# Decoder block on one core: narrow attention heads on quarters of the TensorE array

## The chip, the cores and the metric

The kernel runs on one core of one Trainium2 chip. The metric is device microseconds of one execution. The kernel before takes 4916.42 us (median of 3 runs, 4914.16 to 4921.12).

## The reference

A two-layer decoder over x of shape 4 x 512 x 256 (four batches): attention with 16 heads of 64, layer norm, attention of x against a context with 16 heads of 16 and a mask, layer norm, a mixture of 8 experts, layer norm, a four-layer state-space scan, layer norm, a second cross-attention with 8 heads of 32, and a quantized gated network. The change touches only the two cross-attentions. Their core, cut from the reference (all in float32):

```python
# first cross-attention: H = 16, D_K = 16
q = proj(query, Wq, bq); k = proj(key, Wk, bk); v = proj(key, Wv, bv)
scores = einsum('bhqd,bhkd->bhqk', q + pos_bias, k + pos_bias) / sqrt(D_K)
scores = where(m == 0, -1e9, scores)
out = einsum('bhqk,bhkd->bhqd', softmax(scores), v)
# second cross-attention: H = 8, d = 32
a = softmax(einsum('bhnd,bhmd->bhnm', qh, kh) / sqrt(d))
ca = einsum('bhnm,bhmd->bhnd', a, vh)
```

## The kernel before, in words

All engines run hand-written programs that meet in semaphores. For each batch the kernel does three attention passes with one routine, `attend`, written once for each engine: pass A (16 heads of 64, 32 steps), pass B (16 heads of 16, padded to 32, 32 steps), and, late in the kernel, pass E (8 heads of 32, 16 steps). The passes A and B of the four batches lie in the first 1.4 ms, those of E in the last 0.8 ms. The experts and the scan lie between.

One step is two heads and one tile of 128 queries against all 512 keys. On TensorE (`attend` at L1034) step i issues, in this order: the scores of step i (L1046, two products of 128 queries by 512 keys into two PSUM banks, `PS[:, 2 * (i % 2) + q]`), the eight 128x128 transposes of the probabilities of step i - 3 (L1058), and the value products of step i - 7 (L1075). In pass B and E (`per == 4`) a head has 32 rows and 32 columns. Its scores are still computed with 64 rows of the array: q is stored twice (`pj_q`, L731 to L738), once with the odd and once with the even 32-row strips set to zero, so that one 64-row product gives one head. The two heads of a step use rows 0 to 63 and 64 to 127. The value products of a head write 32 of the 128 columns (`p0`), over 512 queries, for one chunk c of 128 keys:

```python
for q in range(2):
    h = head(j, q, per)
    p0 = h % per * wide
    ins = pe.matmul(PS[p0:p0 + wide, 6 + bank % 2, :], V[:, c, h * wide:(h + 1) * wide],
                    pT[j % 2][:, q, c, :], start=c == 0, stop=c == 3)
```

The other engines in step i: VectorE (`attend` at L1437) takes the row maximum of the scores (pass B: two masked reductions L1451 that also copy the scores into `b_S`, then `nm` at L1454; pass E: one reduction L1459), copies half of the transposed probabilities of step i - 3 out of PSUM bank 4 (L1466) and takes the reciprocal of the sums of step i - 1 (L1477). ScalarE (`attend` at L744) takes the two exponentials of step i (L754) and copies the other half, bank 5, of step i - 3 (L764). GpSimd multiplies the probabilities by the reciprocals (L590). The order is fixed by hand: each engine runs these in the order named, and waits where its input is missing. TensorE waits for `probs_ok` of step i - 2 before the scores, for `scaled` (GpSimd) and for `pt_a`, `pt_v` (both copies of the step before) before the transposes. ScalarE waits for `smax` (L1454 or L1459) before the exponentials, and for the transposes before its copy.

Before a pass, TensorE projects q (L1022) and ScalarE writes it to SBUF: with `pj_q` in two activations for each of 4 (B) or 2 (E) tiles. The first scores of the pass wait for the last of them. After the pass VectorE copies the last bank (L1483) and TensorE goes on with transposes (L1131) or the output projection (L1030).

Of the kernel before, what the change touches and what calls it, by code (L numbers as in the profile page):

```python
# [25 lines left out]
P = 128  # L26
# [73 lines left out]
def decoder(nc, d, out):  # L100
# [11 lines left out]
    with ExitStack() as ctx:  # L112
# [34 lines left out]
        rden = sb("rden", [P, 4, 2])  # L147
        strip01 = sb("strip01", [P, 2])
        qs_b = sb("qs_b", [P, 2])
        qs_e = sb("qs_e", [P, 2])  # L150
        qb_b = sb("qb_b", [P, 2, 4])
        qb_e = sb("qb_e", [P, 2, KC])
        from80 = sb("from80", [P, 1])
# [211 lines left out]
        def head(j, q, per):  # L365

            return 2 * j + q if per == 2 else 4 * (j // 2) + j % 2 + 2 * q

# [347 lines left out]
        def _(act):  # L716
# [13 lines left out]

            def pj_q(b, u, qT, c, nc, scale, bias):  # L731


                act.wait_ge(pj_ps, PJ(b, u) + 1)
                for k in range(2):
                    ins = act.activation(qT[:, k * nc + c, :], PS[:, u % 4, :], ACT.Identity,
                                         bias=bias[:, k, c:c + 1], scale=scale[:, k:k + 1])
                ins.then_inc(pj_ev, 1)  # L738

            def ln(b, i):  # L740
                act.wait_ge(ln_mv, LN(b, i) + 1)
                act.activation(std[:], mv[:, :, 1], ACT.Sqrt, bias=epsc[:, 0:1]).then_inc(ln_std, 1)

            def attend(b, at, n, src, zero_key, probs, pT):  # L744
                s0, g0 = AT(b, at), GT(b, at // 4)
                for i in range(n + LAG):
                    if i < n:
                        s = s0 + i
                        act.wait_ge(smax, s + 1)
                        if i >= 4:  # L750
                            act.wait_ge(pt_ps, s - 3)
                            act.wait_ge(den_ok, s - 3)
                        for q in range(2):
                            ins = act.activation(probs[:, i % 4, q, :], src(i, q), ACT.Exp,  # L754
                                                 bias=nm[:, i % 4, q:q + 1], accum_out=sm[:, i % 4, q:q + 1])
                        if zero_key:
                            ins = act.activation(e0[:, i % 4, :], nm[:, i % 4, :], ACT.Exp)
                        ins.then_inc(probs_ok, 1)
                    k = i - LAG
                    if k >= 0:  # L760
                        act.wait_ge(pt_ps, s0 + k + 1)
                        if k % 4 == 0 and k >= 8:
                            act.wait_ge(av, g0 + k // 4 - 1)
                        act.activation(pT[k // 4 % 2][:, 1, :, k % 4 * P:(k % 4 + 1) * P],  # L764
                                       PS[:, 5, :].rearrange("p (c q) -> p c q", q=P), ACT.Copy).then_inc(pt_a, 1)

# [16 lines left out]
            def attention(b):  # L783
                attend(b, AT_A, 32, lambda i, q: PS[:, 2 * (i % 2) + q, :], True, probs, pT)
# [7 lines left out]
                attend(b, AT_B, 32, lambda i, q: b_S[:, i % 2, q, :], False, probs, pT)  # L792
                ln(b, 1)
                tr_ev(TR_LNB, XT[:, 0, :], b)
# [170 lines left out]
            with act.Fori(0, B) as b:  # L965
# [10 lines left out]
                for c in range(KC):  # L976
                    pj_q(b, PJ_EQ + c, s_qT, c, KC, qs_e, qb_e)
                attend(b, AT_E, 16, lambda i, q: PS[:, 2 * (i % 2) + q, :], False, e_probs, e_pT)
                ln(b, 5)
# [23 lines left out]
        def _(pe):  # L1003
# [29 lines left out]

            def attend(b, at, n, qT, kT, V, per, ot, probs, pT, between=None):  # L1034
                s0, g0, o0 = AT(b, at), GT(b, at // 4), OT(b, ot)
                wide = 64 if per == 2 else 32
                for i in range(n + LAG + 4):
                    if i < n:
                        s, t = s0 + i, i % T
                        if i >= 2:  # L1040
                            pe.wait_ge(probs_ok, s - 1)
                        for q in range(2):
                            h = head(i // T, q, per)
                            r = 64 * q
                            part = h % 2 * (qT.shape[1] // 2) if per == 4 else 0
                            ins = pe.matmul(PS[:, 2 * (i % 2) + q, :],  # L1046
                                            qT[r:r + 64, part + h // per, t * P:(t + 1) * P],
                                            kT[r:r + 64, h // per, :], start=True, stop=True)
# [12 lines left out]
                    if k == n and between is not None:  # L1061
                        between()
                    x = i - LAG - 4
                    if x >= 0:
                        j, c = x // 4, x % 4
                        bank = j if per == 2 else j // 2
                        if c == 0:
                            pe.wait_ge(pt_a, s0 + 4 * j + 4)
                            pe.wait_ge(pt_v, s0 + 4 * j + 4)
# [35 lines left out]
            def attention(b):  # L1105
# [7 lines left out]

                attend(b, AT_A, 32, a_qT, a_kT, a_V, 2, OT_A, probs, pT, keys)
                for t in range(T):
# [11 lines left out]
                pe.wait_ge(tm_ev, TM.one(b, TM_SA))  # L1127
                attend(b, AT_B, 32, b_qT, b_kT, b_V, 4, OT_B, probs, pT)
                for t in range(T):
# [170 lines left out]
            with pe.Fori(0, B) as b:  # L1300
# [26 lines left out]
                pe.wait_ge(tm_ev, TM.two(b, TM_MHA))  # L1327
                attend(b, AT_E, 16, s_qT, s_kT, s_V, 4, OT_E, e_probs, e_pT)
                for t in range(T):
# [43 lines left out]
        def _(v):  # L1373
            v.wait_ge(ld_const, 64)
            for g in range(4):
                for k in range(2):
                    v.memset(strip01[32 * g:32 * g + 32, k:k + 1], 1.0 if g % 2 == k else 0.0)

            v.wait_ge(act_set, 1)
# [7 lines left out]
            v.wait_ge(r_init, 5)  # L1387
            for k in range(2):
                v.tensor_scalar(qb_b[:, k, :], cols[:, C_BQ:C_BQ + 4], strip01[:, k:k + 1], None, ALU.mult)
                v.tensor_scalar(qb_e[:, k, :], cols[:, C_QB:C_QB + KC], strip01[:, k:k + 1], None, ALU.mult)  # L1390
            v.tensor_scalar(qs_b[:], strip01[:], 0.25, None, ALU.mult)
            v.tensor_scalar(qs_e[:], strip01[:], 32.0 ** -0.5, None, ALU.mult).then_inc(dve_set, 1)
            v.wait_ge(dve_set, 1)
# [43 lines left out]
            def attend(b, at, n, own, per, ot, zero_key, out_T, masked, pT):  # L1437
                s0, g0 = AT(b, at), GT(b, at // 4)
                for i in range(n + LAG + 5):
                    s = s0 + i  # L1440
                    if i < n:
# [4 lines left out]
                        if masked:  # L1446
# [3 lines left out]
                            for q in range(2):  # L1450
                                ins = v.tensor_tensor_reduce(b_S[:, i % 2, q, :], PS[:, 2 * (i % 2) + q, :], b_neg[:, i % T, :],  # L1451
                                                             1.0, -3.0e38, ALU.add, ALU.max, mx[:, i % 4, q:q + 1])
# [9 lines left out]
                    if 0 <= k < n:  # L1462
                        v.wait_ge(pt_ps, s0 + k + 1)
                        if k % 4 == 0 and k >= 8:
                            v.wait_ge(av, g0 + k // 4 - 1)
                        v.tensor_copy(pT[k // 4 % 2][:, 0, :, k % 4 * P:(k % 4 + 1) * P],  # L1466
                                      PS[:, 4, :].rearrange("p (c q) -> p c q", q=P)).then_inc(pt_v, 1)
                    k = i - 1
# [432 lines left out]
```

## Time and profile before

| | us |
|---|---|
| median of 3 runs | 4916.42 |
| profiled execution | 4919.05 |
| its span, first to last instruction | 4917.4 |
| TensorE busy | 4034.2 (82%) |
| VectorE busy | 3272.3 (67%) |
| ScalarE busy | 2190.4 (45%) |
| GpSimd busy | 2323.4 (47%) |
| mean granted TensorE clock | 0.924 |

The profiled execution is 2.6 us above the median, and 1.65 us of it lie outside the span. A product in float32 appears as two MATMUL records of its form, each with its weight load (PEld); a transpose appears as one. The busy time of matmuls is modelled at their ends, so the start of the next group is the better measure of what a group costs. [...]

### The profile page before, as it was taken

To read this page: it belongs to the slowest core of one execution; us is meant where nothing else is said; L and a number is where in the kernel's file an instruction comes from. 1 tells how busy PE (TensorE), PEld (TensorE's weight loads), DVE (VectorE), ACT (ScalarE), POOL (GpSimd) and SP (SyncE) were. 2 spreads that over 40 slices of the span, in tenths; PEclk is the share of its full clock that TensorE was granted. 3 is DMA by queue.
4 is the path that set the end of the run, shared out by engine and by line. 5 is a ranking of instruction groups with operands and counts; after the bars stand their busy time and mean duration, and the time that the engine had idled before them with its cause. 6 is when DMAs were issued, how large, how long until landed. Compare 5 with 4: busy or idle time off the path is not lost.

```text
span 4917.4 us, 47718 instructions
## 1 busy us (share of the span) xinstructions
PE 4034.2 (82%) x14992; PEld 2056.3 (42%) x14992; DVE 3272.3 (67%) x4305; ACT 2190.4 (45%) x4097; POOL 2323.4 (47%) x1202
## 2 busy tenths in 40 slices
PE   7888888888869995888888888888889866776766
PEld 3433443444359992333333333333333323333433
DVE  3555446445631114999999999999999995454454
ACT  3444445434522224555555545555555542242332
POOL 2344334324410006777777777777777773120210
PEclk9999999999979996999999999998999999887988
DMA  5000000000068862111111111111111111000000
GB/s 205 18 5 10 18 14 1 18 14 9 1 240 319 311 267 78 33 31 36 41 33 35 33 42 31 35 33 42 31 38 34 33 60 37 1 13 13 0 5 4
DMA packets 102371, 272.72 MB, mean 55 GB/s; under 512 B 9776, under 2 KB 55728, under 8 KB 96400
## 3 DMA queue, kind: packets, MB, share of 16 engines
q1 hardware_dynamic: 97216, 256.75, 15.3%
q0 software_dynamic: 4944, 13.51, 0.8%
q8 instruction: 90, 1.47, 0.1%
q14 instruction: 121, 0.99, 0.1%
HBM read 237.32 MB, written 32.90 MB: 55 GB/s over the span
## 4 chain that ended last, share of the span: by engine, by line
PE 55%; POOL 15%; issue 13%; DVE 10%; ACT 4%; SPq 1%; DMA 1%; POOLq 0%; DVEq 0%; ACTq 0%
POOL AR L697 10%; PE PS L1278 7%; PE PS L1075 6%; PE PS L1058 6%; PE PS L1046 6%; PE PS L1171 6%; PE PS L1022 5%; PE PS L1030 4%; PE PS L1223 4%; PE PS L1181 3%; PE PS L1198 2%; DVE AR L1717 2%; POOL AR L655 1%; DVE PS L1711 1%; ACT AR L754 1%
## 5 line engine op out<-in xcount | busy, mean ns | idle before, releaser
L697 POOL TENSOR_TENSOR AR<-AR 128x1024 f32<-128x1024 f32 x512 | 1205.6, 2357 | 557.4 <-DVE AR L1717 543.1
L590 POOL TENSOR_TENSOR AR<-AR,rden 128x1024 f32<-128x1024 f32 x320 | 605.7, 1893 | 1292.5 <-DVE rden L1477 1226.3
L1278 PE MATMUL PS<-AR,ident 128*128 128x512 f32 x2048 | 1078.6, 653 | 165.8 <-POOL AR L697 165.7
L1717 DVE TENSOR_TENSOR_SCAN AR<-AR,PS 128x1024 f32<-128x1024 f32 x512 | 1170.3, 2286 | 19.0 <-ACT AR L929 1.4
L929 ACT ACTIVATE AR<-AR,mcol 128x511 f32<-128x511 f32 x1024 | 667.8, 711 | 116.2 <-DVE AR L1717 65.7
L1711 DVE TENSOR_TENSOR PS<-AR,PS 128x1024 f32<-128x1024 f32 x512 | 628.6, 1228 | 57.7 <-PE PS L1264 23.1
L1278 PEld LDWEIGHTS PS<-AR,ident 128*128 128x128 f32 x2048 | 384.1, 201 | 670.9 <-issue 385.9
L1058 PE MATMUL PS<-ident,AR 128*128 128x128 f32 x2560 | 344.7, 278 | 122.2 <-issue 68.3
L1058 PEld LDWEIGHTS PS<-ident,AR 128*128 128x128 f32 x2560 | 276.5, 141 | 381.5 <-issue 361.7
L1046 PE MATMUL PS<-AR 64*128 64x512 f32 x1280 | 363.2, 648 | 54.2 <-ACT AR L754 24.0
L754 ACT ACTIVATE AR<-PS,nm 128x512 f32<-128x512 f32 x384 | 260.4, 683 | 291.9 <-DVE nm L1457 227.5
L1075 PE MATMUL PS<-AR 128*32 128x512 f32 (+1 forms) x1280 | 331.7, 608 | 0.0
L1022 PE MATMUL PS<-AR 128*128 128x512 f32 x608 | 295.7, 645 | 20.8 <-DVE AR L1406 10.7
L1171 PE MATMUL PS<-AR 128*128 128x128 f32 x2496 | 287.8, 277 | 8.5 <-ACT AR L811 8.5
L1171 PEld LDWEIGHTS PS<-AR 128*128 128x128 f32 x2496 | 287.4, 193 | 10.8 <-ACT AR L811 8.9
L1030 PE MATMUL PS<-AR 128*128 128x256 f32 (+1 forms) x896 | 241.2, 429 | 45.4 <-DVE AR L1508 18.0
L1451 DVE CUSTOM_DVE_ANT_0 AR<-PS,AR 128x512 f32<-128x512 f32 x256 | 166.7, 689 | 166.6 <-PE PS L1046 146.7
L1198 PE MATMUL PS<-AR 128*128 128x512 f32 x512 | 263.7, 640 | 6.3 <-ACT AR L866 2.1
L1466 DVE COPY AR<-PS 128x512 f32<-128x512 f32 x320 | 220.0, 687 | 73.0 <-PE PS L1058 71.8
L754 ACT ACTIVATE AR<-AR,nm 128x512 f32<-128x512 f32 x256 | 182.6, 714 | 175.1 <-DVE nm L1454 174.9
L1223 PE MATMUL PS<-AR 128*128 128x512 f32 x512 | 240.4, 593 | 3.0 <-ACT AR L870 2.3
L1656 DVE TENSOR_TENSOR AR<-PS,AR 128x512 f32<-128x512 f32 x78 | 53.9, 691 | 271.9 <-ACT AR L820 271.9
(254 smaller groups left out, 4836.7 us busy)
## 6 DMA issues: line engine op xcount, KB each, us to landing
AR<-in_xw SPq DMA_DIRECT2D x39, 3072.0 KB, 10.4
AR<-mid_cs SPq DMA_DIRECT2D x256, 256.0 KB, 3.3
mid_xs<-AR SPq DMA_DIRECT2D x32, 512.0 KB, 7.8
AR<-mid_xs SPq DMA_DIRECT2D x39, 128.0 KB, 9.6
mid_ys<-AR POOLq DMA_DIRECT2D x39, 128.0 KB, 7.9
AR<-in_ctx SPq DMA_DIRECT2D x8, 512.0 KB, 5.1
AR<-in_mask SPq DMA_DIRECT2D x4, 1024.0 KB, 5.4
mid_x<-AR SPq DMA_DIRECT2D x8, 512.0 KB, 3.0
```

The costliest lines, as they stand in the source:

```text
L590: pool.tensor_tensor(probs[:, i % 4], probs[:, i % 4], rden[:, i % 4, :].rearrange("p (q o) -> p q o", o=1).to_broadcast([P, 2, 512]), ALU ...
L697: pool.tensor_tensor(m_HC[:, W % 3], m_H[:, W % 3, :].rearrange("p (c s) -> p c s", c=2), m_cb[:, n % 4:n % 4 + 1, :].to_broadcast([P, 2, ...
L754: ins = act.activation(probs[:, i % 4, q, :], src(i, q), ACT.Exp, bias=nm[:, i % 4, q:q + 1], accum_out=sm[:, i % 4, q:q + 1])
L929: ins = act.activation(m_dA[:, W % 4, c, 1:512], m_dl[i % 2][:, cc, 1:512], ACT.Exp, scale=mcol[:, i // B, at:at + 1])
L1022: ins = pe.matmul(PS[:, u % 4, :], w[:, k, c * P:(c + 1) * P], xT[:, k, :], start=k == 0, stop=k == kc - 1)
L1046: ins = pe.matmul(PS[:, 2 * (i % 2) + q, :], qT[r:r + 64, part + h // per, t * P:(t + 1) * P], kT[r:r + 64, h // per, :], start=True, stop ...
L1058: ins = pe.transpose(PS[:, 4 + q, c * P:(c + 1) * P], probs[:, k % 4, q, c * P:(c + 1) * P], ident[:])
L1075: ins = pe.matmul(PS[p0:p0 + wide, 6 + bank % 2, :], V[:, c, h * wide:(h + 1) * wide], pT[j % 2][:, q, c, :], start=c == 0, stop=c == 3)
L1171: ins = pe.matmul(PS[:, bank, f * P:(f + 1) * P], w[:, kc, f0:f0 + P], x_T[:, kc, :], start=kc == 0, stop=kc == KC - 1)
L1278: ins = pe.matmul(PS[:, 2 * hf + c, :], ident[:], m_HC[:, W % 3, c, :], start=False, stop=n == NS - 1)
L1711: v.tensor_tensor(PS[:, 4:6, :], m_du[i % 2][:, 2 * hf:2 * hf + 2, :], PS[:, 6:7, :].to_broadcast([P, 2, 512]), ALU.mult).then_inc(d_bx, 1)
L1717: v.tensor_tensor_scan(m_H[:, W % 3, :], m_dA[:, W % 4].rearrange("p c s -> p (c s)"), PS[:, 4:6, :].rearrange("p c s -> p (c s)"), 0.0, A ...
```

## The change

1. The heads of a narrow pass are taken in another order: steps i and i + 1 are now the four heads of one quarter set at the same query tile (`step_of`). For `per == 4` TensorE issues the scores of steps i and i + 1 together at even i, four products with 32 rows each, one for each quarter of the array's rows and one for each of the four PSUM banks, and none at odd i.
2. Before such a group TensorE waits for the step i - 1 (instead of i - 2): in pass B for `smax`, since VectorE's copy frees the bank, in pass E for `probs_ok`.
3. The value products of one issue are four, one for each quarter of the columns, over 256 queries (two tiles) instead of two over 512. The buffer pT is viewed as 4 heads x 4 chunks x 256 queries for this (`part_of`), and both copies write into this view.
4. q is no longer stored twice: `pj_q` and its zero strips are gone, and q is written by one activation for each tile (`pj`).
5. Some tiny VectorE instructions of the set-up of those strips are gone. Pass A keeps its instructions and its order.

```diff
         def head(j, q, per):
-            return 2 * j + q if per == 2 else 4 * (j // 2) + j % 2 + 2 * q
+            return 2 * j + q
+        def step_of(i, per):
+            return (i // T, i % T) if per == 2 else (2 * (i // 8) + i % 2, i % 8 // 2)
+        def part_of(pT, k, q, per):
+            j, t = step_of(k, per)
+            if per == 2:
+                return pT[k // 4 % 2][:, q, :, t * P:(t + 1) * P]
+            quad = pT[k // 4 % 2].rearrange("p a c n -> p (a c n)").rearrange("p (h c n) -> p h c n", h=4, c=4)
+            return quad[:, 2 * (j % 2) + q, :, t % 2 * P:(t % 2 + 1) * P]
...
-            def pj_q(b, u, qT, c, nc, scale, bias):
-                act.wait_ge(pj_ps, PJ(b, u) + 1)
-                for k in range(2):
-                    ins = act.activation(qT[:, k * nc + c, :], PS[:, u % 4, :], ACT.Identity,
-                                         bias=bias[:, k, c:c + 1], scale=scale[:, k:k + 1])
-                ins.then_inc(pj_ev, 1)
...
-                    pj_q(b, PJ_BQ + c, b_qT, c, 4, qs_b, qb_b)
+                    pj(b, PJ_BQ + c, b_qT[:, c, :], ACT.Identity, 0.25, cols[:, C_BQ + c:C_BQ + c + 1])
...
                     if i < n:
-                        s, t = s0 + i, i % T
-                        if i >= 2:
+                        s = s0 + i
+                        free = smax if masked else probs_ok
+                        if per == 2 and i >= 2:
                             pe.wait_ge(probs_ok, s - 1)
-                        for q in range(2):
-                            h = head(i // T, q, per)
-                            r = 64 * q
-                            part = h % 2 * (qT.shape[1] // 2) if per == 4 else 0
-                            ins = pe.matmul(PS[:, 2 * (i % 2) + q, :],
-                                            qT[r:r + 64, part + h // per, t * P:(t + 1) * P],
-                                            kT[r:r + 64, h // per, :], start=True, stop=True)
-                        ins.then_inc(scores, 1)
+                        if per == 4 and i % 2 == 0 and i >= 2:
+                            pe.wait_ge(free, s)
+                        for e in ((i,) if per == 2 else (i, i + 1) if i % 2 == 0 else ()):
+                            j, t = step_of(e, per)
+                            for q in range(2):
+                                h = head(j, q, per)
+                                r = h % per * wide
+                                ins = pe.matmul(PS[:, 2 * (e % 2) + q, :], qT[r:r + wide, h // per, t * P:(t + 1) * P],
+                                                kT[r:r + wide, h // per, :], start=True, stop=True)
+                            ins.then_inc(scores, 1)
...
-                        for q in range(2):
-                            h = head(j, q, per)
-                            p0 = h % per * wide
-                            ins = pe.matmul(PS[p0:p0 + wide, 6 + bank % 2, :], V[:, c, h * wide:(h + 1) * wide],
-                                            pT[j % 2][:, q, c, :], start=c == 0, stop=c == 3)
+                        for q in range(per):
+                            h = per * bank + q
+                            p0 = q * wide
+                            n0 = 0 if per == 2 else u % 2 * 256
...
+                            ins = pe.matmul(PS[p0:p0 + wide, 6 + bank % 2, n0:n0 + 1024 // per], V[:, c, h * wide:(h + 1) * wide],
+                                            moved[:, q, c, :], start=c == 0, stop=c == 3)
```

TensorE's program in pass B of the kernel before, steps 5 to 7 (L1046 scores, L1058 transposes, L1075 value products; the REGISTER_ALU rows keep the semaphore counts):

```order
L1041 REGISTER_ALU
L1046 MATMUL PS<-AR 128x512 x2
L1058 MATMUL PS<-ident,AR 128x128 x8
L1041 REGISTER_ALU
L1046 MATMUL PS<-AR 128x512 x2
L1058 MATMUL PS<-ident,AR 128x128 x8
L1075 MATMUL PS<-AR 32x512 x2
L1041 REGISTER_ALU
L1046 MATMUL PS<-AR 128x512 x2
L1058 MATMUL PS<-ident,AR 128x128 x8
L1075 MATMUL PS<-AR 32x512 x2
```

The same place in the changed kernel (L1047 scores, L1058 transposes, L1078 value products):

```order
L1041 REGISTER_ALU
L1047 MATMUL PS<-AR 128x512 x4
L1058 MATMUL PS<-ident,AR 128x128 x8
L1052 REGISTER_ALU
L1058 MATMUL PS<-ident,AR 128x128 x8
L1078 MATMUL PS<-AR 32x256 x4
L1041 REGISTER_ALU
L1047 MATMUL PS<-AR 128x512 x4
L1058 MATMUL PS<-ident,AR 128x128 x8
L1078 MATMUL PS<-AR 32x256 x4
```

Every second step has lost its scores, and the step before it issues four. A value issue has four products of 256 instead of two of 512. The transposes stand where they stood.

ScalarE's program ahead of pass B, kernel before (writing q, with the semaphores waited for):

```order
L736 ACTIVATE AR<-PS,qb_b,qs_b 128x512 [waits pj_ps]
L736 ACTIVATE AR<-PS,qb_b,qs_b 128x512
L734 REGISTER_ALU
L736 ACTIVATE AR<-PS,qb_b,qs_b 128x512 [waits pj_ps]
L736 ACTIVATE AR<-PS,qb_b,qs_b 128x512
L749 REGISTER_ALU
L754 ACT_TABLE_LOAD
```

The changed kernel there:

```order
L736 ACTIVATE AR<-PS,cols 128x512 [waits pj_ps]
L735 REGISTER_ALU
L736 ACTIVATE AR<-PS,cols 128x512 [waits pj_ps]
L747 REGISTER_ALU
L752 ACT_TABLE_LOAD
```

One activation for each projected tile is left of two. The table load for the exponentials still follows the last of them.

## Rows read from the trace of the kernel before

**Rows 1.** The page: the group of the score products, all passes.

```profile
L1046 PE MATMUL PS<-AR 64*128 64x512 f32 x1280 | 363.2, 648 | 54.2 <-ACT AR L754 24.0
```

**Rows 2.** Whole passes B, E: length; PE, PEld, DVE, ACT, POOL busy; PEclk, DMA.

```profile
568.10:685.70 117.60, 98.90 (x513) 42.22 (x513) 73.19 (x228) 66.83 (x162) 60.57 (x32) 1.00 0.00 1
4757.40:4815.00 57.60, 49.58 (x258) 21.85 (x259) 32.60 (x50) 33.53 (x82) 30.29 (x16) 1.00 0.00 0
```

**Rows 3.** Chain that ended last, pass B: start, us, what.

```profile
600.67 1.06 PE PS L1046 x4
601.73 0.56 issue
602.30 1.06 PE PS L1058 x8
603.36 0.98 PE PS L1075 x4
...
605.40 0.20 issue
...
607.65 1.06 PE PS L1046 x4
```

**Rows 4.** Timeline, pass B, from the scores at 604.27 to the transposes at 609.29.

```profile
604.27 1.13 PE L1046 MATMUL PS<-AR 64*128 64x512 f32 x4
...
605.64 0.69 DVE L1451 CUSTOM_DVE_ANT_0 AR<-PS,AR 128x512 f32<-128x512 f32 x1 [1.48 <-PE PS L1046]
...
607.19 0.72 ACT L754 ACTIVATE AR<-AR,nm 128x512 f32<-128x512 f32 x1 [1.69 <-DVE nm L1454]
...
608.61 0.57 ACT L764 ACTIVATE AR<-PS 128x512 f32<-128x512 f32 x1
...
609.29 1.06 PE L1058 MATMUL PS<-ident,AR 128*128 128x128 f32 x8 [0.58 <-issue]
```

**Rows 5.** Chain that ended last, pass E.

```profile
4790.15 1.06 PE PS L1046 x4
...
4796.59 1.06 PE PS L1046 x4
```

**Rows 6.** Timeline of TensorE: second scores of a pass B, first and second of E.

```profile
572.58 1.13 PE L1046 MATMUL PS<-AR 64*128 64x512 f32 x4 [2.46 <-ACT AR L754]
...
4757.40 1.99 PE L1046 MATMUL PS<-AR 64*128 64x512 f32 x8 [1.62 <-ACT AR L736]
4761.33 1.13 PE L1046 MATMUL PS<-AR 64*128 64x512 f32 x4 [1.95 <-ACT AR L754]
```

**Rows 7.** Timeline of TensorE, the value products that end a pass E.

```profile
4809.07 4.57 PE L1075 MATMUL PS<-AR 128*32 128x512 f32 x20
```

**Rows 8.** Writing q (line L736), and a group of L729, one activation with a bias.

```profile
L736 ACT ACTIVATE AR<-PS,qb_b,qs_b x32: 768/774/779, 219.8 to 1243.5; 128x512 f32<-128x512 f32 x32
...
L729 ACT ACTIVATE AR<-PS,cols 128x512 f32<-128x512 f32 x64 | 44.0, 687 | 117.9 <-PE PS L1022 117.9
```

**Rows 9.** Stretches at the start of four passes (A, B, A, B); columns as in rows 2.

```profile
409.80:419.80 10.00, 7.59 (x28) 3.11 (x28) 6.78 (x14) 5.18 (x17) 3.78 (x2) 0.83 0.01 2
568.10:578.10 10.00, 6.31 (x28) 2.46 (x28) 7.16 (x24) 6.31 (x14) 3.78 (x2) 1.00 0.00 1
749.50:759.50 10.00, 6.40 (x28) 2.54 (x28) 7.23 (x14) 5.09 (x16) 3.78 (x2) 1.00 0.01 2
907.00:917.00 10.00, 7.07 (x26) 3.17 (x28) 6.27 (x23) 5.99 (x14) 3.79 (x2) 0.83 0.00 1
```

**Rows 10.** Timeline of TensorE in the last of those stretches.

```profile
911.45 1.13 PE L1046 MATMUL PS<-AR 64*128 64x512 f32 x4 [2.46 <-ACT AR L754]
913.05 1.93 PE L1046 MATMUL PS<-AR 64*128 64x512 f32 x4 [0.47 <-ACT AR L754]
914.91 1.93 PE L1058 MATMUL PS<-ident,AR 128*128 128x128 f32 x8
916.76 1.13 PE L1046 MATMUL PS<-AR 64*128 64x512 f32 x4
```

More of the change, by code:

```diff
@@ L147, in decoder @@
         rden = sb("rden", [P, 4, 2])
[L148 to L152, printed above, removed]
         from80 = sb("from80", [P, 1])
@@ L742, in ln, with attend @@
                 act.activation(std[:], mv[:, :, 1], ACT.Sqrt, bias=epsc[:, 0:1]).then_inc(ln_std, 1)
-            def attend(b, at, n, src, zero_key, probs, pT):
+            def attend(b, at, n, src, per, probs, pT):
                 s0, g0 = AT(b, at), GT(b, at // 4)
@@ L763, in attend @@
                             act.wait_ge(av, g0 + k // 4 - 1)
-                        act.activation(pT[k // 4 % 2][:, 1, :, k % 4 * P:(k % 4 + 1) * P],
-                                       PS[:, 5, :].rearrange("p (c q) -> p c q", q=P), ACT.Copy).then_inc(pt_a, 1)
+                        act.activation(part_of(pT, k, 1, per), PS[:, 5, :].rearrange("p (c q) -> p c q", q=P), ACT.Copy).then_inc(pt_a, 1)
             def project(b, prior=None):
@@ L783, in attention @@
             def attention(b):
-                attend(b, AT_A, 32, lambda i, q: PS[:, 2 * (i % 2) + q, :], True, probs, pT)
+                attend(b, AT_A, 32, lambda i, q: PS[:, 2 * (i % 2) + q, :], 2, probs, pT)
                 for c in range(4):
@@ L976, in _ @@
                 for c in range(KC):
-                    pj_q(b, PJ_EQ + c, s_qT, c, KC, qs_e, qb_e)
-                attend(b, AT_E, 16, lambda i, q: PS[:, 2 * (i % 2) + q, :], False, e_probs, e_pT)
+                    pj(b, PJ_EQ + c, s_qT[:, c, :], ACT.Identity, 32.0 ** -0.5, cols[:, C_QB + c:C_QB + c + 1])
+                attend(b, AT_E, 16, lambda i, q: PS[:, 2 * (i % 2) + q, :], 4, e_probs, e_pT)
                 ln(b, 5)
@@ L1032, in tm, with attend @@
                 ins.then_inc(tm_ps, 1)
-            def attend(b, at, n, qT, kT, V, per, ot, probs, pT, between=None):
+            def attend(b, at, n, qT, kT, V, per, ot, masked, probs, pT, between=None):
                 s0, g0, o0 = AT(b, at), GT(b, at // 4), OT(b, ot)
@@ L1064, in attend @@
                     if x >= 0:
-                        j, c = x // 4, x % 4
-                        bank = j if per == 2 else j // 2
+                        u, c = x // 4, x % 4
+                        bank = u if per == 2 else u // 2
                         if c == 0:
-                            pe.wait_ge(pt_a, s0 + 4 * j + 4)
-                            pe.wait_ge(pt_v, s0 + 4 * j + 4)
+                            pe.wait_ge(pt_a, s0 + 4 * u + 4)
+                            pe.wait_ge(pt_v, s0 + 4 * u + 4)
                             if bank >= 2:
                                 pe.wait_ge(o_sb, o0 + bank - 1)
-                        for q in range(2):
-                            h = head(j, q, per)
-                            p0 = h % per * wide
-                            ins = pe.matmul(PS[p0:p0 + wide, 6 + bank % 2, :], V[:, c, h * wide:(h + 1) * wide],
-                                            pT[j % 2][:, q, c, :], start=c == 0, stop=c == 3)
+                        for q in range(per):
+                            h = per * bank + q
+                            p0 = q * wide
+                            n0 = 0 if per == 2 else u % 2 * 256
+                            moved = (pT[u % 2] if per == 2 else
+                                     pT[u % 2].rearrange("p a c n -> p (a c n)").rearrange("p (h c n) -> p h c n", h=4, c=4))
+                            ins = pe.matmul(PS[p0:p0 + wide, 6 + bank % 2, n0:n0 + 1024 // per], V[:, c, h * wide:(h + 1) * wide],
+                                            moved[:, q, c, :], start=c == 0, stop=c == 3)
                         if c == 3:
@@ L1112, in keys @@
                         pj(b, PJ_BK + c, wbk, CT, c)
-                attend(b, AT_A, 32, a_qT, a_kT, a_V, 2, OT_A, probs, pT, keys)
+                attend(b, AT_A, 32, a_qT, a_kT, a_V, 2, OT_A, False, probs, pT, keys)
                 for t in range(T):
@@ L1127, in attention @@
                 pe.wait_ge(tm_ev, TM.one(b, TM_SA))
-                attend(b, AT_B, 32, b_qT, b_kT, b_V, 4, OT_B, probs, pT)
+                attend(b, AT_B, 32, b_qT, b_kT, b_V, 4, OT_B, True, probs, pT)
                 for t in range(T):
@@ L1327, in _ @@
                 pe.wait_ge(tm_ev, TM.two(b, TM_MHA))
-                attend(b, AT_E, 16, s_qT, s_kT, s_V, 4, OT_E, e_probs, e_pT)
+                attend(b, AT_E, 16, s_qT, s_kT, s_V, 4, OT_E, False, e_probs, e_pT)
                 for t in range(T):
@@ L1374, in _ @@
             v.wait_ge(ld_const, 64)
-            for g in range(4):
-                for k in range(2):
-                    v.memset(strip01[32 * g:32 * g + 32, k:k + 1], 1.0 if g % 2 == k else 0.0)
             v.wait_ge(act_set, 1)
@@ L1387, in _ @@
             v.wait_ge(r_init, 5)
[L1388 to L1392, printed above, removed]
+            v.sem_inc(dve_set, 1)
             v.wait_ge(dve_set, 1)
```

9 lines of the change are left out of this document (4 added, 5 removed).

## The prediction

> **What bounds the kernel now.** [...] The four passes B and four passes E are 700 us of the 4919.05; all else should stay. So the question is what a TensorE saving is worth inside a pass. The chain of waits answers it [rows 3]: two steps of pass B are scores 1.06, issue 0.56, transposes 1.06, values 0.98, scores 1.06, issue 0.20, transposes 1.06, values 0.98 = 6.98 us from 600.67 to 607.65. The two "issue" pieces are TensorE waiting ahead of the transposes. The timeline tells for what [rows 4]: scores start at 604.27, VectorE's reductions at 605.64, the exponentials at 607.19, ScalarE's copy L764 at 608.61, and 0.11 us after that copy has ended (609.18) the transposes start. From the scores to those transposes are 5.02 us, in which TensorE has a whole step of other work (1.06 + 0.98 + 1.06) and then waits. The period is this loop: 5.0 from scores to the next step's transposes, then 0.98 to 1.06 of transposes and 0.98 of values, and the scores of two steps later. Three of its parts belong to other engines. The reader is to see that TensorE is 6.2 of 6.98 us busy and yet that its work lies on the path only in part.
>
> **The change, part by part, against 4919.05.**
>
> *Scores.* Two groups of 1.06 become one group of four. The two products of a group run abreast: a record lasts 0.648 on the mean [rows 1], and the four of a group take 1.06 in all [rows 3]. I take 1.06 for four products as well; it can't be less than that, and two groups run apart would be 2.12. The removed group stood in the part of the loop where TensorE waits anyway, so alone it is worth nothing in the steady round; it turns into waiting.
>
> *Value products.* 0.98 for 512 columns in the middle of the stream; back to back, 20 records (five issues) take 4.57, the last four issues about 0.86 each [rows 7]. Half the columns stream in 0.43; with the 0.12 that an issue costs between other work, 0.55. Ends: 0.49 (half of 0.98) and 0.98 (the number of columns counts for nothing). One of the two issues in a round is in the loop. So the new loop of B is 5.02 + 0.99 + 0.55 = 6.56 us for two steps, 0.43 less than 6.98. VectorE is busy 73.19 / 32 = 2.3 us a step, ScalarE 2.1, GpSimd 1.9 [rows 2], so 4.6, 4.2 and 3.8 of the 6.56: none becomes the bound. The new wait for `smax` of step i - 1 is over before TensorE comes to it: 1.37 from scores to reductions and 1.55 for these and their negation [rows 4], some 0.8 of copy and reciprocal, 1.5 for the second reductions make 5.2, and the next group is due at 6.56. Pass E: 6.44 for two steps, from 4790.15 to 4796.59, becomes 6.0 by the same step [rows 5].
>
> *Whole passes.* B has 16 rounds, of which 12 are in the steady rhythm: 12 x 0.43 = 5.2. At the end of a pass nothing hides TensorE: the last scores fall away (1.06), and four value issues back to back are 0.43 shorter each: 2.8. The start of B is neutral: the second group waited for the first exponentials (2.46 idle [rows 6]) and now comes as late. Together 8.0, four times: 32 us. In E the second group starts 3.93 after the first [rows 6], now it must wait for the exponentials of the other step too, 1.4 (0.7 each, as in [rows 4]), of which I take 1.2, and so again in the next round: 2.4 lost. Three steady rounds give 1.3, the end 2.8: net 1.7, four times: 7 us.
>
> *Writing q.* The first scores wait for two activations of 0.774 behind the last projection; now for one of 0.687 [rows 8]: 0.86 less, eight times: 7 us. The removed activations of the other tiles lie beside the projections, the few set-up instructions beside the first loads: nothing.
>
> Sum so far: 32 + 7 + 7 = 46 us less.
>
> *What comes back: the clock.* In the new round of B TensorE works 1.06 + 0.99 + 0.55, then stands still for about 2.3 us until the copy frees the transposes, then works 1.54. Such a wait exists before only at the start of a pass, and there the clock answers: of four starts with an idle stretch of 2.2 to 2.5 us, two show a granted clock of 0.83 over 10 us and two show 1.00 [rows 9]. [...] I take 1.2. How often: half of the idle stretches of this size led to it, but a slowed round has no such idle stretch; so one in four of the 64 rounds of B, 16. In the steady rounds of E the wait is only about 1.8, and at 1.95 (the start of E) the clock held, so I count only the start of E, with an idle stretch of 4 us and one more behind it: 2 for a pass, 8. Together 24 x 1.2 = 29 us. Bounds: 8 of them (10 us) and one in almost every round, some 56 x 1.5 = 84 us.
>
> [...]
>
> Net: -46 + 29 = -17, from 4919.05 to 4902. The median lies 2.6 below the profiled execution: 4900.
>
> **The rivals.**
> 1. *The clock holds in pass B.* For it: half the starts held, and all steady rounds before did. Against: 64 new idle stretches. Then only E's starts cost 10: -36, 4880.
> 2. *The clock falls in nearly every round* (slower than before). The place is TensorE behind its wait for the ScalarE copy; price 1.5 for each fall, as more of the slowed work is then on the path; 84 us: 4954. It decides from 46 / 1.2 = 38 falls on, of some 96 rounds. Against it: a slowed group fills its own idle time.
> 3. *Quarters stream no faster by halving the columns*, since eight weight loads and eight products in an issue bound it: values stay at 0.98. That takes back 0.43 x (12 + 3) x 4 = 26 and 0.43 x 4 x 8 = 14 us; TensorE then waits less, some 10 falls: -46 + 40 + 12 = +6, 4922. For it: no group of the trace issues as densely. Against: the score groups already hold several records at a time, 0.648 each in 1.06 for four [rows 1, 3].
> 4. *Four quarters don't run abreast*, only two and two: 2.12 for a score group, all of the added 1.06 in the loop, 0.98 for values: 7.9 for a round, about +95 with the ends, less 7 for q: 5005. Against it: the two halves run abreast now [rows 1, 3]. [...]
>
> **How the numbers follow.** Chances: the forecast 0.46, rival 1 0.27, rival 2 0.12, rival 3 0.09, rival 4 0.03, 0.03 for else. The number is the likeliest case, 4900. Its own range is 4886 to 4916 (14 to 36 falls). With rival 1, down to 4872 (no fall at all, values at 0.49), and the lower part of rival 2 and rival 3, the range is 4872 to 4934. A measurement of this kernel can tell 0.2%, 10 us. Faster by more (below 4906.6): rival 1 and about 0.8 of the forecast, 0.64. Within: the rest of the forecast, half of rival 3, a part of rival 2: 0.20. Slower: 0.16.
>
> **What would show it.** Right: score groups of eight records with about 1.06 to the next start; value issues at 0.55; the wait ahead of every second transposes about 2.3 in B, put down to ScalarE's copy; rounds of 6.5 to 6.6 in B and 6.0 in E where the clock is 1.00; a granted clock of 0.90 to 0.97 over passes B; E's second group 5.2 after its first; one activation ahead of the first scores. Wrong: value issues over 0.7, score groups near 2.1, or rounds at full clock that are held by `smax`, `probs_ok` or `scaled`. The prediction of the time fails if the low stretches are fewer than 14 or more than 36.

## The result and the profile after

| | before | changed |
|---|---|---|
| median of 20 runs, us | 4916.41 | 4925.99 |
| lowest to highest, us | 4910.01 to 4921.28 | 4909.88 to 4934.17 |
| span of the profiled execution, us | 4917.4 | 4926.5 |
| mean granted TensorE clock | 0.924 | 0.906 |

The ratio is 1.0019, with a 95% interval of 1.0012 to 1.0026: the change makes the kernel slightly slower. The prediction said 4900 with a chance of 0.64 for faster.

The page of the changed kernel, its engines and the three groups that the change is about (scores L1047, transposes L1058, value products L1078):

```profile
PE 3919.0 (80%) x15752; PEld 2066.7 (42%) x15760; DVE 3298.5 (67%) x4291; ACT 2171.5 (44%) x4073; POOL 2325.4 (47%) x1202
...
L1058 PE MATMUL PS<-ident,AR 128*128 128x128 f32 x2560 | 381.6, 297 | 227.3 <-ACT AR L762 191.3
...
L1047 PE MATMUL PS<-AR 32*128 32x512 f32 (+1 forms) x1280 | 282.7, 731 | 68.6 <-ACT AR L752 25.4
...
L1078 PE MATMUL PS<-AR 128*32 128x256 f32 (+1 forms) x2048 | 261.5, 464 | 2.3 <-DVE AR L1461 1.2
```

The group of the transposes on the page of the kernel before:

```profile
L1058 PE MATMUL PS<-ident,AR 128*128 128x128 f32 x2560 | 344.7, 278 | 122.2 <-issue 68.3
```

TensorE is busy 115 us less than before (4034.2), and none of it is in the time. The idle time ahead of the transposes has gone from 122 to 227 us, 191 of it ended by ScalarE's copy (L762), while the mean score record rose from 648 ns [rows 1] to 731 ns: some ran at a granted clock of 0.50, where a group takes 2.02 to the next start (4766.63 to 4768.65, below) for 1.07 to 1.10.

The timeline of TensorE in a pass B of the changed kernel, steady rounds (a round is two steps, from one score group to the next):

```profile
602.92 1.14 PE L1047 MATMUL PS<-AR 32*128 32x512 f32 x8
604.02 1.07 PE L1058 MATMUL PS<-ident,AR 128*128 128x128 f32 x8
605.01 0.64 PE L1078 MATMUL PS<-AR 128*32 128x256 f32 x8
607.93 1.07 PE L1058 MATMUL PS<-ident,AR 128*128 128x128 f32 x8 [2.28 <-ACT AR L762]
608.93 0.64 PE L1078 MATMUL PS<-AR 128*32 128x256 f32 x8
609.50 1.14 PE L1047 MATMUL PS<-AR 32*128 32x512 f32 x8
...
614.50 1.94 PE L1058 MATMUL PS<-ident,AR 128*128 128x128 f32 x8 [2.27 <-ACT AR L762]
616.37 1.08 PE L1078 MATMUL PS<-AR 128*32 128x256 f32 x8
617.39 1.29 PE L1047 MATMUL PS<-AR 32*128 32x512 f32 x8
```

Eight records of four score products take 1.10 from start to start (602.92 to 604.02): the quarters run abreast. A value issue takes 0.57 (608.93 to 609.50). The round at full clock (a granted clock of 1.00 from 602.90 to 609.50) is 609.50 - 602.92 = 6.58 us, where it was 6.98 [rows 3], with the wait of 2.28 for ScalarE's copy in it. The next round, from 609.50 to 617.39, takes 7.89: behind the wait the clock is down (0.50 from 614.40 to 617.40), and the transposes take 1.87 to the next start.

Pass E starts worse (timeline of TensorE, changed kernel; compare [rows 6]):

```profile
4761.36 1.14 PE L1047 MATMUL PS<-AR 32*128 32x512 f32 x8 [0.85 <-ACT AR L736]
4766.63 2.09 PE L1047 MATMUL PS<-AR 32*128 32x512 f32 x8 [4.13 <-ACT AR L752]
4768.65 1.97 PE L1058 MATMUL PS<-ident,AR 128*128 128x128 f32 x8
4772.85 2.09 PE L1047 MATMUL PS<-AR 32*128 32x512 f32 x8 [2.23 <-ACT AR L752]
4774.87 1.97 PE L1058 MATMUL PS<-ident,AR 128*128 128x128 f32 x8
4778.27 1.94 PE L1058 MATMUL PS<-ident,AR 128*128 128x128 f32 x8 [1.43 <-ACT AR L762]
```

After an idle stretch of 4.13 us everything runs at a granted clock of 0.50, and it stays so until 4782, over three score groups (the row from 4764.90 below). The stretches by pass (four passes B, one pass E; columns as in [rows 2]):

```profile
224.40:343.60 119.20, 80.89 (x647) 44.93 (x648) 80.29 (x229) 66.94 (x162) 60.63 (x32) 0.89 0.00 1
563.10:682.00 118.90, 78.96 (x648) 43.46 (x649) 80.17 (x229) 66.89 (x162) 60.62 (x32) 0.90 0.00 1
902.50:1022.00 119.50, 80.46 (x640) 44.08 (x640) 79.75 (x228) 66.84 (x162) 60.62 (x32) 0.87 0.00 1
1241.20:1360.00 118.80, 79.71 (x640) 43.96 (x640) 79.60 (x228) 66.91 (x162) 60.63 (x32) 0.89 0.00 1
...
4761.40:4822.00 60.60, 41.26 (x321) 22.95 (x321) 31.77 (x50) 33.27 (x82) 30.28 (x16) 0.83 0.00 0
```

A mean clock of 0.89 over 119 us is 26 us at half clock, a granted clock of 0.50. Two of the low stretches by themselves, the first of a pass B and the first of a pass E:

```profile
566.50:576.70 10.20, 7.23 (x30) 3.73 (x31) 6.15 (x22) 6.03 (x17) 5.68 (x3) 0.50 0.00 1
4764.90:4782.00 17.10, 11.62 (x48) 6.26 (x48) 7.12 (x12) 8.93 (x25) 8.45 (x5) 0.50 0.00 0
```

By the clock's records it falls 22 times in the four passes B, for 109 us together, and twice in each pass E, for 17.1 and 3.4 us: 30 low stretches and 191 us. Before there were two of 3.4 us, one in each of two passes B, and none in E. Pass E went from the 57.1 us between its first scores and the work behind it (4757.40 to 4814.50) to 60.5 (4761.36 to 4821.90). The first pass E begins at 4157.0 where it began at 4162.2. From there to the end the changed kernel loses 14 us, and the four passes E alone are 14 us longer, by the table below.

How long the passes are, from the first scores to the end of the last value products by the timelines, and how much of them was at half clock (a granted clock of 0.50); the experiments that the lower rows belong to follow:

| kernel | four passes B, us | four passes E, us | at half clock, us |
|---|---|---|---|
| before | 468.7 | 224.8 | 7 |
| changed | 472.5 | 238.7 | 191 |
| e1_single | 469.5 | 242.3 | 218 |
| e2_fill | 440.2 | 219.6 | 0 |
| e6_rows64 | 442.4 | 210.4 | 10 |
| e7_small | 480.7 | 245.2 | 154 |
| e9_starts | 457.2 | 224.8 | 61 |

### The profile page after: what moved, and what is told of

Read it like the earlier page. It is cut to its first block, busy times and chain, and to the rows that moved or that the text cites. A ratio compares the mean times of both kernels' runs of the same rounds, so it can differ in the third digit from the quotient of the medians.

```text
span 4926.5 us, 49210 instructions
## 1 busy us (share of the span) xinstructions
PE 3919.0 (80%) x15752; PEld 2066.7 (42%) x15760; DVE 3298.5 (67%) x4291; ACT 2171.5 (44%) x4073; POOL 2325.4 (47%) x1202
## 4 chain that ended last, share of the span: by engine, by line
issue 36%; POOL 28%; PE 27%; DVE 6%; ACT 1%; SPq 1%; POOLq 0%; DMA 0%; DVEq 0%; ACTq 0%
POOL AR L597 12%; POOL AR L704 10%; PE PS L1281 7%; PE PS L1174 6%; PE PS L1226 4%; PE PS L1184 3%; DVE AR L1711 2%; PE PS L1201 2%; DVE PS L1705 1%; POOL AR L662 1%; POOL AR L657 1%; POOL AR L653 1%; SPq L433 1%; PE PS L1278 1%; PE PS L1019 1%
## 5 line engine op out<-in xcount | busy, mean ns | idle before, releaser
L1705 DVE TENSOR_TENSOR PS<-AR,PS 128x1024 f32<-128x1024 f32 x512 | 628.5, 1228 | 57.1 <-PE PS L1267 23.6
L1058 PE MATMUL PS<-ident,AR 128*128 128x128 f32 x2560 | 381.6, 297 | 227.3 <-ACT AR L762 191.3
L1058 PEld LDWEIGHTS PS<-ident,AR 128*128 128x128 f32 x2560 | 306.0, 153 | 462.7 <-issue 420.3
L1047 PE MATMUL PS<-AR 32*128 32x512 f32 (+1 forms) x1280 | 282.7, 731 | 68.6 <-ACT AR L752 25.4
L1027 PE MATMUL PS<-AR 128*128 128x256 f32 (+1 forms) x896 | 239.4, 427 | 45.4 <-DVE AR L1502 18.0
L1078 PE MATMUL PS<-AR 128*32 128x256 f32 (+1 forms) x2048 | 261.5, 464 | 2.3 <-DVE AR L1461 1.2
```

The source lines that it names most:

```text
L1058: ins = pe.transpose(PS[:, 4 + q, c * P:(c + 1) * P], probs[:, k % 4, q, c * P:(c + 1) * P], ident[:])
L1705: v.tensor_tensor(PS[:, 4:6, :], m_du[i % 2][:, 2 * hf:2 * hf + 2, :], PS[:, 6:7, :].to_broadcast([P, 2, 512]), ALU.mult).then_inc(d_bx, 1)
```

## The experiments

Each ratio is to the kernel before, timed beside the experiment on the same chip: 4923.8 us for the first four (e1, e2, e4, e5), 4918.3 for the next three (e6, e7, e8), 4923.3 for the last (e9).

### Scores step by step again (e1_single)

```diff
-                        if per == 2 and i >= 2:
+                        single = True
+                        if single and i >= 2:
                             pe.wait_ge(probs_ok, s - 1)
...
-                        for e in ((i,) if per == 2 else (i, i + 1) if i % 2 == 0 else ()):
+                        for e in ((i,) if single else (i, i + 1) if i % 2 == 0 else ()):
```

> The changed kernel, but with the scores of each step issued by themselves again (two quarter products at every step, wait for probs_ok of step i - 2, as before), values in quarters kept. Theory 'clock': pairing the scores only turned TensorE work into waiting, and the waiting let the clock fall. Then rounds stay at 6.6 us in B and about 6.0 in E, the clock over passes B and E is back at 0.98 to 1.00, starts of E as in the kernel before, and the time is 4865 to 4880 us, faster than both kernels. Rival 'order': what costs is something else of the change (the new order of heads, the copies into the new view, column quarters); then it stays at 4905 to 4930.

Measured: 4936.6 us, ratio 1.0020 (0.9998 to 1.0042). Neither expectation held. The steady rounds of B are 6.56 us, as 'clock' has them, but the clock is down in the passes for 218 us, more than the 191 of the changed kernel: pairing is not all that lets it fall. The starts of three groups in pass E (timeline of TensorE of this experiment):

```profile
4772.19 2.08 PE L1048 MATMUL PS<-AR 32*128 32x512 f32 x4
4774.19 1.97 PE L1059 MATMUL PS<-ident,AR 128*128 128x128 f32 x8
4776.09 2.08 PE L1048 MATMUL PS<-AR 32*128 32x512 f32 x4
4778.10 1.97 PE L1059 MATMUL PS<-ident,AR 128*128 128x128 f32 x8
4780.00 2.08 PE L1048 MATMUL PS<-AR 32*128 32x512 f32 x4
```

TensorE has no idle time in these rows and runs at a granted clock of 0.50 (10.00 us busy of the 10.00 from 4772.00). The same stretch of 27 us near the start of pass B, busy time and clock, in this experiment:

```profile
571.60:598.90 27.30, 27.22 (x94) 13.34 (x92) 15.12 (x48) 14.24 (x38) 13.64 (x8) 0.50 0.00 1
```

and in the kernel before:

```profile
571.60:598.90 27.30, 20.37 (x107) 9.44 (x108) 18.78 (x62) 17.96 (x47) 16.79 (x9) 1.00 0.00 1
```

Busy 27.22 of 27.30 us at a clock of 0.50, against 20.37 at 1.00. A wait stands at the head of it here as there, 3.30 us ahead of the scores at 571.16 where it was 2.46 [rows 6], and that can be why the clock falls; it can't be why it stays down, as TensorE then idles 0.08 us in 27.30. The kernel before shows what a fall costs it: with 2.46 us of idle ahead of the scores at 911.45, its 64-row scores and transposes were slow from 913.05 to 916.76, at a granted clock of 0.51 (913.30 to 916.70), and the scores at 916.76 took 1.13 again for the 1.93 of those at 913.05 [rows 10]. What differs in those stretches is the form of the scores: two products on 32 rows each, half of the array, where the kernel before uses 64 rows for each head, half of them multiplied by zeros, and so the whole array. (The order of heads and the view that the copies write to differ as well.) In both passes the low stretch ends soon after the value products have come in, which fill the array with four quarters of the columns. In pass B they come at 592.44 and 597.36, and the scores at 598.37 take 1.28 to the next start where those at 593.45 took 2.01. In pass E:

```profile
4787.81 1.08 PE L1079 MATMUL PS<-AR 128*32 128x256 f32 x8
...
4792.73 1.08 PE L1079 MATMUL PS<-AR 128*32 128x256 f32 x8
4793.74 1.16 PE L1048 MATMUL PS<-AR 32*128 32x512 f32 x4
```

The granted clock is 0.50 from 4787.80 to 4793.70 and 1.00 from 4793.80 to 4800.

### Zero products where TensorE waits (e2_fill)

```diff
+                def keep(i, times):
+                    nx = i - LAG - 4
+                    bk = max(nx, 0) // 8
+                    fresh = nx <= 0 or nx % 4 == 0
+                    n0 = max(nx, 0) // 4 % 2 * 256
...
+                    for _ in range(times):
+                        pe.matmul(PS[:, 6 + bk % 2, n0:n0 + P], zw[:], ones[:], start=fresh, stop=fresh)
...
+                        if per == 4 and i % 2 and i < n:
+                            keep(i, 8)
                         pe.wait_ge(scaled, s0 + k + 1)
```

> The changed kernel with products by a zero weight tile (128 columns of ones) that add nothing, put where TensorE waits in passes B and E: 8 ahead of every second transposes, 12 and 6 ahead of the second and third score group. Theory 'clock': more TensorE work makes it faster; clock 0.98 to 1.00 in passes B and E, rounds 6.6 and 6.0, and 4875 to 4895 us. Rival 'waits': if the new waits (probs_ok of step i - 1, the burst of four) are what costs, the extra work changes nothing or costs: 4925 to 4945.

Measured: 4871.7 us, ratio 0.9891 (0.9839 to 0.9943). 848 added products, 214 us of TensorE work that computes nothing, make the changed kernel faster by some 1.3%, from a ratio of 1.0019 to 0.9891. Whole passes B and E of it:

```profile
558.00:668.50 110.50, 102.13 (x916) 69.91 (x916) 79.87 (x228) 66.81 (x162) 60.58 (x32) 1.00 0.01 1
4711.90:4770.00 58.10, 53.35 (x478) 38.18 (x479) 32.44 (x52) 33.15 (x82) 30.28 (x16) 1.00 0.00 0
```

The clock is 1.00 throughout, and the rounds of B are 6.57 us. The eight passes take 659.8 us together, where the changed kernel takes 711.2 and the kernel before 693.5: the low clock costs the changed kernel 51 us, and its other steps give 34. That refutes the rival 'waits'. The span of this experiment is 48 us shorter than before (4869.4 for 4917.4); 14 of them lie outside the passes, 6 in the writing of q, and of the rest at least a part where other work happens to meet the full clock (a projection ahead of a pass E, L1028, takes 1.99 us at a granted clock of 1.00 here, for the 3.63 us at 0.54 of L1027 in the changed kernel). Differences of that size between two kernels say nothing about the passes.

### Only pass E step by step (e4_single_e)

```diff
+                        single = per == 2 or not masked
```

> The changed kernel with the scores of pass E issued step by step again, pass B left paired. Theory 'clock': E loses 20.5 us of low clock in each pass and its late start, some 6 to 7 us for each of four passes; 4897 to 4905 us, with B's rounds and clock as in the changed kernel (0.87 to 0.90). Rival 'only the start of E' (its wait for probs_ok, not the clock): 2.4 us for each of four passes, 4914 to 4918.

Measured: 4930.6 us, ratio 1.0008 (0.9985 to 1.0031). Neither expectation held, for the reason seen in the first experiment: the early groups of pass E here take 3.91 us for one step, at a granted clock of 0.50 (4379.20 to 4387.00). The 70 us from 20 us ahead of the second pass E on have a clock of 0.78:

```profile
4350.00:4420.00 70.00, 59.91 (x272) 30.90 (x270) 37.26 (x67) 32.12 (x79) 25.32 (x14) 0.78 0.00 0
```

### Value products issued twice (e5_twice)

```diff
-                        for q in range(per):
+                        for m, q in ((m, q) for m in range(per // 2) for q in range(per)):
```

This is e1_single with more work in the value issues; the lines are set against the changed kernel.

> Scores step by step in both passes and every value product in quarters issued twice (the values come out doubled). It puts a value issue back to about 1.0 to 1.1 us. If the saving of the first experiment is the value issues' (0.43 in each round and at the ends), it is gone: rounds of 7.0 to 7.1 in B, and 4910 to 4925 us (the 7 us of writing q stay). If it comes from the order of heads or the waits, it stays below 4890.

Measured: 4962.9 us, ratio 1.0073 (1.0049 to 1.0096). The steady rounds of B are 3.08 + 3.91 = 6.99 us where the first experiment has 2.66 + 3.90 = 6.56, as expected of the value issue. The time missed the expectation, with 195 us of the passes at half clock here too. Against the first experiment it is 26 us more. It shows that a value issue lies in the loop.

### The value products alone, scores on 64 rows (e6_rows64)

```diff
-                                r = h % per * wide
-                                ins = pe.matmul(PS[:, 2 * (e % 2) + q, :], qT[r:r + wide, h // per, t * P:(t + 1) * P],
-                                                kT[r:r + wide, h // per, :], start=True, stop=True)
+                                r = 64 * q
+                                part = h % 2 * (qT.shape[1] // 2) if per == 4 else 0
+                                ins = pe.matmul(PS[:, 2 * (e % 2) + q, :], qT[r:r + 64, part + h // per, t * P:(t + 1) * P],
+                                                kT[r:r + 64, h // per, :], start=True, stop=True)
```

with `pj_q`, its strips and the old pairs of heads in a step put back, and the first experiment's issue at every step. The new order of steps and the view of pT stay.

> The kernel before with one part of the change alone: the value products in quarters (four of 256 columns at an issue). Scores as before, 64 rows of the array for each head, two products at every step, q stored twice. [...] Theory 'rows': TensorE's clock goes with how much of the array the scores use, and 64-row products on both halves bring it back: rounds 6.57 in B and 6.03 in E, clock 0.98 to 1.00 in passes B and E, 4875 to 4885 us (40 us less: 6.6 and 3.4 for a pass). Rival 'value quarters': if the shorter value issues themselves let the clock fall, it falls here too, 4900 us or more.

Measured: 4875.1 us, ratio 0.9907 (0.9890 to 0.9923), as expected. Scores of three steps in pass E, which make a round of 6.03 us, timeline of TensorE, and whole passes B and E:

```profile
4754.41 1.13 PE L1061 MATMUL PS<-AR 64*128 64x512 f32 x4
...
4757.28 1.13 PE L1061 MATMUL PS<-AR 64*128 64x512 f32 x4
4758.88 1.07 PE L1072 MATMUL PS<-ident,AR 128*128 128x128 f32 x8 [0.47 <-issue]
4759.87 0.64 PE L1092 MATMUL PS<-AR 128*32 128x256 f32 x8
4760.44 1.13 PE L1061 MATMUL PS<-AR 64*128 64x512 f32 x4
```

```profile
560.20:671.00 110.80, 87.20 (x640) 43.08 (x640) 72.80 (x227) 66.80 (x162) 60.60 (x32) 0.98 0.00 1
4723.00:4777.00 54.00, 43.32 (x323) 22.10 (x324) 32.96 (x50) 33.51 (x82) 30.29 (x16) 1.00 0.00 0
```

This is one part of the change, and the passes are shorter with it than in any other kernel here: pass B 110.8 us for 117.6, pass E 54.0 for 57.6 [rows 2], 652.8 us for all eight. Where the clock falls in them (three times in B, never in E) it is back after 3.4 us (0.51 from 564.80 to 568.20, 1.00 from 571 on). From the first experiment it differs in the rows of the scores (and in the head order and the writing of q that go with them). TensorE is busy less (87.2 us in a pass B, 99.2 in the first experiment's 120.8) and the clock is 0.98 instead of 0.89.

### The zero products on 32 rows (e7_small)

```diff
-                        pe.matmul(PS[:, 6 + bk % 2, n0:n0 + P], zw[:], ones[:], start=fresh, stop=fresh)
+                        pe.matmul(PS[:, 6 + bk % 2, n0:n0 + P], zw[0:32, :], ones[0:32, :], start=fresh, stop=fresh)
```

> The second experiment (zero products where TensorE waits), each of them on 32 rows instead of 128: as many, as long, a quarter of the array. Theory 'idle time alone' (TensorE busy or not is what counts): as in the second experiment, 4870 to 4880 us, clock 0.98 to 1.00 in the passes. Theory 'rows': the clock falls in the passes as in the changed kernel or nearly, 4905 to 4935 us.

Measured: 4924.2 us, ratio 1.0013 (1.0003 to 1.0022). The same number of products, as long at the same clock (16 records in 2.05 us), in the same places as in the second experiment, and 52 us slower. Steady rounds at full clock, up to one that falls (timeline of TensorE), and the whole pass:

```profile
976.60 1.14 PE L1061 MATMUL PS<-AR 32*128 32x512 f32 x8
977.70 1.07 PE L1074 MATMUL PS<-ident,AR 128*128 128x128 f32 x8
978.70 0.64 PE L1094 MATMUL PS<-AR 128*32 128x256 f32 x8
979.26 2.05 PE L1044 MATMUL PS<-ones,zw 32*128 32x128 f32 x16
981.61 1.06 PE L1074 MATMUL PS<-ident,AR 128*128 128x128 f32 x8 [0.30 <-issue]
982.61 0.64 PE L1094 MATMUL PS<-AR 128*32 128x256 f32 x8
...
985.84 2.05 PE L1044 MATMUL PS<-ones,zw 32*128 32x128 f32 x16
988.18 1.69 PE L1074 MATMUL PS<-ident,AR 128*128 128x128 f32 x8 [0.29 <-issue]
```

```profile
913.00:1033.00 120.00, 113.05 (x916) 77.41 (x916) 79.47 (x227) 67.03 (x163) 60.57 (x32) 0.90 0.00 1
```

TensorE idles 0.30 us in a round and is busy 113 of 120 us, and the clock falls all the same. "Idle time alone" is refuted. It is not nothing either: the passes have 154 us at half clock here, 191 in the changed kernel. At the starts the added products run at a granted clock of 0.50 on the path (16 records at 929.04 take 3.71 to the next start) and cost time themselves (rounds of 9.77 us), so not all of the 52 us is the low clock of the kernel's own work.

### Zero products, and pass E starting step by step (e8_start)

```diff
-                        if per == 2 and i >= 2:
+                        single = per == 2 or (not masked and i < 4)
...
+                        if single and i >= 2:
                             pe.wait_ge(probs_ok, s - 1)
```

> The second experiment with the first two score groups of pass E issued step by step (wait for probs_ok of step i - 2), so that E starts as in the kernel before. If the late start of E costs what its second and third groups show (5.27 and 5.27 instead of 3.93 and 3.94), it is 2.5 us less for each of four passes than the second experiment: 4860 to 4866 us. If the delay is taken up later, 4868 to 4874.

Measured: 4866.5 us, ratio 0.9893 (0.9877 to 0.9910), by the ratio the same as the second experiment. The trace says why: the second and third groups come at 3.93 and 1.33 us, but the next one, the first pair behind them, waits for the step before it, 5.25: 10.51 us from the first group, where the second experiment has 5.27 + 5.27 = 10.54. The kernel before starts the scores of that step after 3.93 + 1.34 + 2.60 = 7.87. The delay belongs to the first pair, wherever it stands, since it waits for the exponentials of the step just before it.

### Zero products at the starts alone (e9_starts)

```diff
-                            keep(i, 8)
+                            keep(i, 0)
```

> The second experiment with the zero products only at the start of passes B and E (12 ahead of the second score group, 6 ahead of the third), none in the steady rounds. In the changed kernel the low stretches of the passes lie mostly at the start: 13.6 to 24 of 24 to 31 us in B, all 20.5 in E. [...] If one start at full clock is enough to hold it for the pass: 4870 to 4876. If the starts don't matter: 4910 or more.

Measured: 4908.3 us, ratio 0.9968 (0.9956 to 0.9980), between the expectations (4876 and 4910). Two passes B of it:

```profile
224.00:343.00 119.00, 81.92 (x678) 46.64 (x679) 80.08 (x228) 66.91 (x162) 60.57 (x32) 0.91 0.00 1
564.40:678.00 113.60, 76.11 (x678) 43.96 (x679) 80.17 (x228) 66.87 (x162) 60.58 (x32) 0.97 0.00 1
```

In the second of them the clock holds until 624 us (1.00 from 564.40). In the first it holds over the two score groups that have zero products ahead of them, and falls at 238.4 (0.50 from there to 241.50), behind a wait of 1.86 us with none. In both, two or more steady rounds fall (7.89 us for 6.57). By the table above the products at the starts shorten the passes by 29 us (711.2 to 682.0), those in the steady rounds by another 22 (to 659.8). By the ratios it is 0.5% and 0.8% (1.0019, 0.9968, 0.9891); a part of the second step, 14 us of 36 between the two spans, lies outside the passes.

## Why the prediction was wrong

The time, 4926.0, lies in the range (4872 to 4934), but on the other side of 4916: slower by 0.19%, where faster had 0.64. By the lengths of the passes and the spans:

| | forecast, us | measured, us |
|---|---|---|
| passes without the clock's part | -39 | -34 (e2_fill against before) |
| writing q | -7 | -6 (8 x 0.77) |
| low clock | +29 | +51 (changed against e2_fill) |
| in all | -17 | +11; +9.1 by the two spans |

- **The loop: right.** Forecast 6.56 us for a round of B and 6.0 of E; 6.57 and 6.03 wherever the clock is full. Score group forecast 1.06, measured 1.07 to 1.10; value issue 0.55, measured 0.57; the wait ahead of the transposes 2.3 (B) and 1.8 (E), measured 2.28 and 1.74, put down to the ScalarE copy as forecast. Removing a score group was worth nothing in the loop: e6_rows64 keeps all of them and has the same rounds.
- **Whole passes: near.** Forecast 8.0 us less for a pass B and 1.7 for E; where the clock is full they are 7.1 and 1.3 less. The late start of E, forecast 2.4, is 2.3: a pass E takes 54.9 us with pairs and 52.6 step by step, both at full clock (e2_fill, e6_rows64).
- **Writing q: right.** The wait ahead of the first scores went from 1.62 to 0.85, 0.77 for 0.86 forecast.
- **The clock: the step that failed, and in it the length of a low stretch.** The forecast had 24 low stretches, 16 in B and 8 in E, each of 3.4 us, and 1.2 us for each: 29 us. The number was near: 30, of which 22 in B and the 8 in E. The price of 3.4 us at half clock was near too: 51 us for 191 are 0.9. But a stretch lasted 6.4 us on the mean, and the first one of a pass E 17.1, five times what was taken. No run shows the 1.2 us that the sum took for a low stretch: the runs gave 51 us for 30 of them, 1.7 each. The forecast counted each fall once because "a slowed round has no such idle stretch": the slowed work was to fill its own idle time and so end the low stretch. At the starts of the passes it did not. With 29 us for 51 the sum came out on the wrong side.
- **The reason under that length was incomplete.** The text took idle time for the cause. e1_single has TensorE busy 27.22 of 27.30 us at half clock; e7_small falls with 0.30 us idle in a round (0.55 from 988.20 to 992.00). The forecast left out that the change also takes work out of the array: the kernel before filled all 128 rows for two score groups a round, zeros and all, the changed kernel for one. With 64 rows for each head every fall within a pass B was over after 3.4 us, in the kernel before and in e6_rows64.
- Rival 2 (the clock falls in nearly every round, slower) had the sign, but not the course: 30 falls, fewer than its deciding 38, and in the steady part of the passes B seven rounds of some 48. The stretches at the starts made up for it. In the steady rounds of E no fall came, as forecast. Rivals 3 and 4 are refuted by the groups' times, rival 1 by the clock.
- That the time lies in the range is no merit of the sum: its own range was 4886 to 4916, and the rest came from the rivals.

What stays open: how much of the fall in the changed kernel itself is due to the idle stretches and how much to the smaller work of the array. Pairing on 32 rows changed both. The runs separate them only in other kernels: idle time filled with 32-row work didn't hold the clock (0.90 over a pass B), filled with 128-row work it did (1.00). Whether the transposes play another part than the other products was not tried: at the starts, where the low stretches were longest (17.1 us in the changed kernel), TensorE had only 32-row scores and transposes to do.

## What to carry to other kernels

Packing narrow products into fewer array passes paid here only where TensorE's time was in the loop: the value issues were (0.41 us in a round; alone, 0.9% of the kernel), the scores were not, and taking them out left an idle, emptier array whose clock fell (0.87 to 0.90 over a pass B). Before such a change, write down which group lies between the last release and the next wait, and change that one alone; read the granted clock of the stretch, not only the busy time, before and after, and in a forecast of the clock ask how long a low stretch will last and not only how often one begins. Zeros multiplied on rows that nobody needs can be the cheaper kernel: with the value products packed in both, scores on 64 rows took 4875.1 us and on 32 rows 4936.6.

## What was not expected of the hardware

- TensorE busy without a gap stayed at half clock in e1_single: 27.22 us of 27.30 at a granted clock of 0.50, with scores on 32 rows for each of two heads and full transposes in turn. With 64 rows for each head, the same rhythm ran at 1.00 in the kernel before, and came back to it after 3.4 us where the clock had fallen.
- Equal numbers of zero products in the same places, equally long at the same clock, on 128 and on 32 rows: 4871.7 and 4924.2 us, clock over a pass B 1.00 and 0.90.
- Idle stretches were followed by a low clock too (0.50 behind a wait of 4.13 us in the changed kernel); the two points above show busy time, in the profile's sense, that didn't bring the clock back or hold it.
